# Moving down products and weight scaling in the feed-forward, and an output product ahead of the values' turn in cross attention

## The reference

```
# layer 0, feed-forward: weights from 4-bit codes, I = 1408
w_gu = dequant_fp4(gate_up_packed, gate_up_scales, 128)
w_down = dequant_fp4(down_packed, down_scales, 128)
gate, up = split(einsum('bsh,oh->bso', x, w_gu))
h = silu(gate) * up
y = einsum('bsi,hi->bsh', h, w_down)
out = y / sqrt(mean(y * y) + 1e-6)

# layer 1, cross attention: 16 heads of 128, 8 key/value heads, context of 512 x 256
q = (x @ Wq), k = (ctx @ Wk), v = (ctx @ Wv)
attn = softmax(q k^T / sqrt(128))
out = (attn v) @ Wo
```

## Time and profile before

| | |
|---|---|
| median of 3 runs | 2464.71 us (2464.12 to 2466.46) |
| the profiled execution | 2463.88 us, span 2461.8 us |
| PE busy | 2366.6 us (96%) |
| PEld busy | 1750.7 us (71%) |
| DVE busy | 1729.6 us (70%) |
| ACT busy | 1195.3 us (49%) |
| POOL busy | 159.0 us (6%) |
| feed-forward, chunks 1 to 10 | about 517 to 847 us |
| cross attention, units | about 1353 to 2330 us |

### The profile page before, as it was taken

One profiled execution on the slowest core, in us unless ns is written; L12 is line 12 of the kernel. 1 busy time (PEld: TensorE's weight loads), 2 busy tenths in 40 slices (PEclk: granted clock), 3 DMA queues, 4 the chain that ended last, 5 costly groups with the idle time before them and its releaser, 6 DMA issues. The chain is left out here.

```text
span 2461.8 us, 37463 instructions
## 1 busy us (share of the span) xinstructions
PE 2366.6 (96%) x11266; PEld 1750.7 (71%) x11266; DVE 1729.6 (70%) x3709; ACT 1195.3 (49%) x2341; POOL 159.0 (6%) x281
## 2 busy tenths in 40 slices
PE   7899998899999899999998999999999999999898
PEld 5655556677777688655557777777777777777677
DVE  6578887778887664666757667676667766667873
ACT  3467765433333522477754544444444444444641
POOL 0000000000000000000022010101000101010200
PEclk9999999999999999999999999999999999999999
DMA  5722201000000134433302000000000000001001
GB/s 164 203 75 71 70 18 69 1 1 0 0 0 0 56 120 156 148 93 100 90 30 73 1 13 9 13 9 13 12 9 13 11 11 17 4 9 45 1 18 52
DMA packets 71922, 110.50 MB, mean 45 GB/s; under 512 B 14266, under 2 KB 25274, under 8 KB 71194
## 3 DMA queue, kind: packets, MB, share of 16 engines
q1 hardware_dynamic: 71834, 109.38, 14.5%
HBM read 75.26 MB, written 34.08 MB: 44 GB/s over the span
## 5 line engine op out<-in xcount | busy, mean ns | idle before, releaser
L3378 DVE SCALAR_TENSOR_TENSOR x_res<-xa_out_bank,xa_den,x_res 128x512 f32 (+1 forms) x256 | 191.6, 748 | 140.3 <-PE xa_out_bank L2853 139.7
L3227 ACT ACTIVATE xa_pT_hi<-xa_t_bank 128x512 fp32r<-128x512 f32 x256 | 149.6, 597 | 127.3 <-PE xa_t_bank L3049 127.3
L327 DVE TENSOR_REDUCE l1s_mx<-l1s_max_bank 128x1 f32<-128x512 f32 x256 | 156.4, 680 | 68.5 <-PE l1s_max_bank L185 68.4
L3238 ACT ACTIVATE xa_prob<-xa_prob,xa_nmax 128x512 f32<-128x512 f32 x256 | 182.6, 715 | 29.1 <-DVE xa_nmax L3345 29.1
L3327 DVE TENSOR_TENSOR xa_pT_lo<-xa_t_bank,xa_pT_hi 128x512 fp32r<-128x512 f32 x256 | 175.6, 687 | 23.6 <-ACT xa_pT_hi L3227 23.4
L327 DVE TENSOR_REDUCE l0s_mx<-l0s_max_bank 128x1 f32<-128x512 f32 x256 | 156.8, 680 | 46.6 <-PE l0s_max_bank L185 46.4
L3345 DVE CUSTOM_DVE_ANT_0 xa_prob<-xa_s_bank,xa_mask_bias 128x512 f32<-128x512 f32 x256 | 171.1, 687 | 22.9 <-PE xa_s_bank L2853 11.3
L3031 PE MATMUL xa_bank_a<-xa_xT_hi,xa_q_w 128*128 (+1 forms) x512 | 181.3, 395 | 0.0
L2853 PE MATMUL xa_out_bank<-xa_o_w,xa_o_hi 128*128 128x512 f32 x512 | 170.9, 415 | 8.4 <-DVE x_res L3378 7.3
L2065 DVE SCALAR_TENSOR_TENSOR ffn_yT<-ffn_y,ffn_ysc,ffn_yT 128x512 f32<-128x512 f32 x164 | 120.4, 745 | 42.6 <-PE ffn_y L1799 42.5
L3049 PE MATMUL xa_t_bank<-ident,xa_prob 128*128 128x128 f32 x1024 | 150.0, 274 | 0.1
(11 more groups left out here) (502 smaller groups left out, 5692.2 us busy)
## 6 DMA issues: line engine op xcount, KB each, us to landing
l0s_q<-l_q SPq DMA_DIRECT2D x96, 128.0 KB, 2.4
l1s_q<-l_q SPq DMA_DIRECT2D x96, 128.0 KB, 3.1
l1s_k<-l_k SPq DMA_DIRECT2D x96, 128.0 KB, 3.2
l0s_k<-l_k SPq DMA_DIRECT2D x96, 64.0 KB, 2.4
x_res<-in_x_dram SPq DMA_DIRECT2D x4, 1024.0 KB, 9.4
l_q<-l_q_hi SPq DMA_DIRECT2D x16, 256.0 KB, 2.6
l_q<-l_q_lo SPq DMA_DIRECT2D x16, 256.0 KB, 3.2
l_q<-l_hi SPq DMA_DIRECT2D x16, 256.0 KB, 2.1
```

Of the source, the lines that this page charges most:

```text
L327: dve.tensor_reduce(self.mx[:, j // QT, j % QT:j % QT + 1], self.max_bank[j % 3][:], AX.X, ALU.max)\
L3227: act.activation(pT_hi[:, kt % (QT - 1), :], t_bank[kt % 2][:], ACT.Copy).then_inc(pT_hi_done, 1)
L3238: act.activation(prob[:, q, :], prob[:, q, :], ACT.Exp, bias=nmax[:, q:q + 1], scale=-1.0, accum_out=den[:, r, 0, q:q + 1]).then_inc(exp_d ...
L3378: dve.scalar_tensor_tensor(xt, out_bank[:], den[:, r, 2, q:q + 1], xt, ALU.mult, ALU.add)\
```

## The change

In the feed-forward, down product 0 comes two gate matmuls later (behind ten), product 1 behind the first two up matmuls, product 2 behind seven up matmuls instead of six; product 3 stays behind the twelfth. The scaling of the next chunk's weights on ACT goes from behind `take_h` of block 0 to behind `silu` of block 1. In the second half of a cross attention unit, output product 1 comes one query matmul earlier, and product 2 goes ahead of the values' turn; DVE adds product 2 ahead of the query's low half.

```diff
                         gate_up(c, s, b, 0, 0, 4)
                         turn_next(0)
-                        gate_up(c, s, b, 0, 4, 8)
+                        gate_up(c, s, b, 0, 4, 10)
                         down_before(0)
                         turn_next(1)
                         finished(0)
-                        gate_up(c, s, b, 0, 8, 12)
+                        gate_up(c, s, b, 0, 10, 12)
+                        gate_up(c, s, b, 1, 0, 2)
                         down_before(1)
                         turn_next(2)
                         finished(1)
                         if b == 3 and more:
                             turn_weights(c + 1, 1)
-                        gate_up(c, s, b, 1, 0, 6)
+                        gate_up(c, s, b, 1, 2, 7)
                         down_before(2)
                         turn_next(3)
                         finished(2)
-                        gate_up(c, s, b, 1, 6, 12)
+                        gate_up(c, s, b, 1, 7, 12)
                         down_before(3)
...
                         silu(c, b)
+                        if b == 1 and more and not first:
+                            scale_weights(c + 1)
                         take_x(2)
...
                         take_h(c, b)
-                        if b == 0 and more and not first:
-                            scale_weights(c + 1)
...
                             next_q(0, 3)
                             out(0)
-                            next_q(3, 9)
+                            next_q(3, 8)
                             out(1)
-                            next_q(9, 12)
+                            next_q(8, 12)
+                            out(2)
                             turn_v(u + 1)
-                            out(2)
                             turn_probabilities(u, r, 0)
...
                         else:
+                            add_last(2)
                             take_q(u + 1, 0)
-                            add_last(2)
                             take_pT(u, r, 0)
```

## The result

The changed kernel takes **2472.15 us** (median of 7 runs, 2469.79 to 2478.18), against 2464.48 us for the kernel before in the runs beside it (7 runs, 2462.23 to 2466.46). The ratio of the two means is 1.0036, 95% interval 1.0026 to 1.0046: slower, by 7.7 us between the medians, and by more than the 0.2% that can be told from no change. Forecast were 2469.8 us and a range from 2459 to 2476.

The account below looks back on a forecast made before the run. TensorE, busy 2366.6 of 2461.8 us, was taken to bound the kernel. Feed-forward -11.2, chunk 0 +1.05 and cross attention +15.0 made +4.9, rounded up to +5.1 on 2464.7: 2469.8 us, range 2459 to 2476.

Parts of the forecast that it names:

- Both feed-forward holes: Feed-forward chunks: TensorE's stalls of 0.34 us in block 1 and 0.91 in block 2 go, 1.22 us a chunk.
- rival 3: Feed-forward: the scaling holds the high copy of block 1, block 2's hole stays whole, 2478 us; chance 0.13.
- The fit at zero reserve in block 1: Feed-forward block 1: down product 0's load, due at 590.95, is allowed at 590.95 too, so the 0.34 us wait goes.
- Chunk 0: First feed-forward chunk: second x turn two matmuls later at half clock delays TensorE, +1.05 us, bounds +0.2 and +2.5.
- Cross attention: Second half of each unit: third turn of probabilities comes 0.49 us later, +15.0 us in all.
- The three zeros: Cross attention unit: earlier second product, third product ahead of the values' turn, and turns filling the fourth's wait each gain 0.
- what is late next: Cross attention unit: ScalarE's values' copy starts later, delaying the first probability copies and third turn of probabilities, +0.49 us.
- DVE's queue: Cross attention unit: bound if only VectorE's sequence of add, queries and first low half of probabilities counts, +0.32 us.
- rival 1: Cross attention: the values' copy costs nothing, slack elsewhere takes up the 0.49; 2454.6 us, chance 0.11.
- Rival 2: Cross attention: the third and fourth products' holes go too, 31 x 0.6 = -18.6 us, 2436; chance 0.03.
- Rival 5: Whole kernel: nothing that shows, feed-forward and cross attention parts both miss, 2464.7 us; chance 0.07.
- Rival 4: Cross attention: the clock falls for a tenth of the stage, 78 us, about 2548 in total; chance 0.02.

Follow-up runs that it names:

- the best kernel here: Against the kernel before: feed-forward edits in chunks 1 to 10, cross attention's output products, turns and copies respaced for the one output bank; 2447.17 us, ratio 0.9928.

## Why the prediction was right, and where it was wrong

It forecast slower (0.49 of the chances) with the time inside the range, 2.4 us under the median measured. In the two traces the touched stages make +6.1 (-10.9, +3.2 and +13.8), where the sum had +4.9, so two misses of opposite sign, in chunk 0 and in cross attention, partly cancel; the other 3.9 of the traces' difference lie in code that wasn't touched. By its own steps:

**Both feed-forward holes: right, with size.** 1.22 us a chunk were forecast, 1.22 measured. Each start in the chain lies within 0.02 us of the one worked out, less 1.36: silu 592.4 (591.02), scaling 592.87 (591.51), hidden product 596.24 (594.90), high copy 596.97 (595.61), load 598.45 (597.10). ScalarE's reserve was 0.21 where 0.25 was forecast, so rival 3, the scaling that holds the high copy, didn't come; by that margin. The fit at zero reserve in block 1 held too.

**Chunk 0: the mechanism right, the term mis-sized.** The forecast was +1.05 us, with +2.5 as the upper bound "if the longer pause brings another stretch at half clock". At equal time at half clock the order costs about 1.13. PE's wait grew by 0.87 (1.57 to 2.44), just the 0.86 that were said to arrive. But the stretch at half clock behind the wait is no bound: it came in four traces of four, and made the term +3.2 in the trace of the changed kernel, +2.5 in its second trace. This is the step that failed, by 1.4 to 2.1 us. How much of the 2.6 between the sum (+5.1) and the median (+7.7) it is can't be told, since stretches that the change doesn't touch moved by more.

**Cross attention: size right, cause incomplete.** The three zeros held: the third product's load 1.41 behind the second's last matmul, no wait before the fourth, 0.83 before the third turn of probabilities (0.8 forecast). The period rose by 0.486 (0.49 forecast), the stage by 13.8 in this pair (15.0 forecast: the last two units, written out, lost 0.15 and 0.28 and not 0.49 each, and the first little), and by 14.5 to 15.6 between the other kernels. The step "what is late next" named the values' copy on ScalarE as what holds the first `pT_hi`. Its own numbers held a second limit that it passed over: the turns of probabilities begin at 1828.66, the fourth starts 0.33 later, the copy 0.31 behind, at **1829.30**, only 0.05 ahead of the 1829.35 that the copy gives. Two limits stood 0.05 apart, and the later one got all of the 0.49. Under both stood the third, which it had as its bound: DVE's queue, +0.32. The kernel with ScalarE's copies exchanged recovered 0.04; the kernel that recovered all of it had the turns, the copies and DVE's order exchanged. The forecast time was safe from the error, but a cure built on it would have failed: exchanging the copies gave 2477.65 us, still 0.51% above before.

**The bounds of the unit.** That only DVE's queue counts (+0.32) and that other slack takes it up (0, rival 1) are excluded by 0.486. Rival 2, all holes gone, wanted a period 0.6 shorter; the best kernel here reached 0.19. Rival 5, nothing, is excluded by the interval.

**Rival 4, the clock in cross attention,** didn't come: in the window from 1820 to 1832 us, with the twelve turns in a row, the granted clock is 1.00, its 2.4 GHz level, and over the whole stage 6.8 us stand at half clock before (3.4 us each at 1354.4 and 2289.6) and 6.8 after (1345.5 and 2294.4). So the prediction's reading that the clock fell only behind the pause before the feed-forward doesn't hold for the whole trace of before, which shows 14 such stretches. The rule of the Trainium skill that spoke for it ("TensorE: Matmul & The Clock Gate", Part 4: PE-mode transpose) is neither borne out nor refuted by that, since the twelve turns are 1.5 us of 12 there. In chunk 0 the clock did fall, behind a wait of 2.44 us; in the 4 us ahead of that wait PE made eight turns and twelve other matmuls.

## What to carry to other kernels

An order that fills one wait moves everything behind it: ask of each moved block what its followers were feeding, since four turns that fill a hole of 0.39 us here held back a chain two engines long by 0.43. Where limits come close to each other, write all of them down (here +0.49, +0.44 and +0.32 to 0.34), because the removal of the last one gains only the difference to the next. And where a pause gets longer at a place at which the granted clock is low nearby, put the further stretch at half clock into the sum and not only into the range.

## What the runs showed of the hardware

- The stretches at half clock in chunk 0 and in cross attention last 3.4 or 6.8 us, and the same code has them at other places in other traces; some stand near the same place in all thirteen, as one that begins at 373 to 378 us. The last stage, identical in all kernels, took 157.5 to 162.2 us in thirteen traces. So a term of 1 or 2 us is read from the stage that it is in and not from the total: 2454.66 and 2454.96 us hid a chunk 0 shorter by 1.7 us.
- The loops themselves repeat closely: the period of the units is 29.93 to 29.95 in the five traces with the order of before, 30.44 or 30.45 in the four with the values' turn moved and ScalarE's order kept, and that of the chunks 31.00 to 31.01 in the six with both feed-forward edits.
- Turns in a row start 0.11 us apart, so that four cost 0.43 us (1826.73 to 1827.16 in the trace of the changed kernel), and all of it shows once they stand in a chain.
- In the second half of a unit the add of the second output product stands 0.55 behind its last matmul, and that of the first 0.67 or 0.68, with DVE idle for 0.28 to 0.48 before it (medians of each of the thirteen traces).
